# Convolution stage of a four-layer graph kernel: one product in split halves, half of an affine map on another engine

## What is computed

```python
x = x + batchnorm(out)                       # end of layer 1; out is the array O below
h = relu(layernorm(x))
h = relu(einsum('ts,bsh->bth', adj, h @ Wg0 + bg0))
h = relu(einsum('ts,bsh->bth', adj, h @ Wg1 + bg1))
...                                          # then the LSTMs over windows, and layer 3
```

## Time and profile before

| | |
|---|---|
| median of three runs | 1221.98 us (1221.71 to 1222.08) |
| profiled execution: its time, its span | 1222.5 us, 1220.8 us |
| busy in the whole span: PE, DVE, ACT, POOL | 97%, 80%, 74%, 35% |
| this stage | from about 319 us to about 466 us of the span |
| busy from 384 to 424 us: PE, DVE, ACT, POOL | 40.00, 34.79, 34.76, 18.43 of 40 us |

### The profile page before, as it was taken

The page is one execution under the profiler, slowest core; times in us unless marked ns, Lnnn a source line. Parts: engine busy times, 40 slices in busy tenths (PEclk is TensorE's granted clock), DMA queues, the critical chain, the costliest instruction groups (busy, mean ns, idle before and its releaser), DMA issues.

```text
span 1220.8 us, 22403 instructions
## 1 busy us (share of the span) xinstructions
PE 1186.0 (97%) x7262; PEld 1023.4 (84%) x7262; DVE 980.9 (80%) x2005; ACT 901.9 (74%) x1733; POOL 428.2 (35%) x794
## 2 busy tenths in 40 slices
PE   8999999989999998999999999999999999989998
PEld 8999988843688886689888988898898899978997
DVE  6888859977688876888788878887887899987774
ACT  5766779978578876877787768776776688875554
POOL 5878748700276430000000000000000377757764
PEclk9999999999999999999999999999999999999999
DMA  8000000000311100000000000000300030001112
GB/s 322 1 2 2 1 1 1 0 1 0 112 62 69 69 35 1 1 1 1 1 1 1 2 1 1 1 1 1 138 1 1 2 139 2 2 1 51 72 70 87
DMA packets 14924, 38.23 MB, mean 31 GB/s; under 512 B 1904, under 2 KB 3952, under 8 KB 13808
## 3 DMA queue, kind: packets, MB, share of 16 engines
q1 hardware_dynamic: 14000, 36.60, 7.9%
q10 hardware_dynamic: 832, 0.46, 0.1%
HBM read 20.27 MB, written 16.78 MB: 30 GB/s over the span
## 4 chain that ended last, share of the span: by engine, by line
PE 53%; DVE 5%; ACT 2%; issue 1%; POOL 1%; POOLq 0%; DVEq 0%; ACTq 0%
PE psum L1197 7%; PE psum L1198 7%; PE psum L1199 7%; PE psum L1216 5%; PE psum L1212 4%; PE psum L1213 4%; PE psum L1484 2%; PE psum L1736 2%; PE psum L1701 2%; PE psum L1490 2%; PE psum L1711 2%; ACT gates L1235 2%; PE psum L1503 1%; PE psum L1504 1%; PE psum L1722 1%; PE psum L1366 1%
## 5 line engine op out<-in xcount | busy, mean ns | idle before, releaser
L1235 ACT ACTIVATE gates<-psum,lstm_bias 128x512 f32<-128x512 f32 (+1 forms) x504 | 302.2, 637 | 101.8 <-PE psum L1216 88.3
L143 POOL TENSOR_TENSOR l2r_sum<-l2r_st 128x8 f32<-128x8 f32 x16 | 5.2, 323 | 518.0 <-DVE l2r_st L116 517.7
L175 ACT ACTIVATE l_h<-X,nmr,rstd 128x128 f32<-128x128 f32 (+1 forms) x392 | 160.6, 484 | 14.6 <-POOLq L169 14.6
L1198 PE MATMUL psum<-lstm_node_hi,Wih_lo 128*128 128x512 f32 (+1 forms) x408 | 148.3, 363 | 0.0
L1197 PE MATMUL psum<-lstm_node_hi,Wih_hi 128*128 128x512 f32 (+1 forms) x408 | 148.1, 363 | 0.0
L1199 PE MATMUL psum<-lstm_node_lo,Wih_hi 128*128 128x512 f32 (+1 forms) x408 | 148.0, 363 | 0.0
L1212 PE MATMUL psum<-lstm_hid_hi,Whh_hi 128*128 128x512 f32 (+1 forms) x288 | 104.7, 363 | 3.9 <-DVE lstm_hid_hi L1295 3.8
L1216 PE MATMUL psum<-lstm_hid_lo,Whh_hi 128*128 128x512 f32 (+1 forms) x288 | 108.0, 375 | 0.0
L1213 PE MATMUL psum<-lstm_hid_hi,Whh_lo 128*128 128x512 f32 (+1 forms) x288 | 103.6, 360 | 0.0
L1240 ACT ACTIVATE gates<-lstm_cell 128x512 f32<-128x512 f32 (+1 forms) x144 | 83.7, 581 | 21.0 <-DVE lstm_cell L1282 20.6
L1197 PEld LDWEIGHTS psum<-lstm_node_hi,Wih_hi 128*128 128x128 f32 x408 | 77.3, 190 | 10.9 <-ACT gates L1235 0.3
(11 more groups left out here) (277 smaller groups left out, 3456.9 us busy)
## 6 DMA issues: line engine op xcount, KB each, us to landing
x_spill<-X SPq DMA_DIRECT2D x32, 256.0 KB, 2.0
X<-x_spill SPq DMA_DIRECT2D x2, 4096.0 KB, 12.3
out<-X SPq DMA_DIRECT2D x32, 256.0 KB, 2.0
X<-in_x SPq DMA_DIRECT2D x6, 1024.0 KB, 15.3
X<-in_x SPq DMA_DIRECT2D x3, 512.0 KB, 8.7
w_raw<-in_WihT SPq DMA_DIRECT2D x1, 1024.0 KB, 5.6
w_raw<-in_WhhT SPq DMA_DIRECT2D x1, 1024.0 KB, 7.8
X<-in_x SPq DMA_DIRECT2D x2, 256.0 KB, 3.2
```

The source lines that it names most:

```text
L175: last = act.activation(h[:, j, :], k.X[:, bass.ds(b0, TB), :][:, j, :], ACT.Relu, bias=k.nmr[:, bass.ds(b0, TB)][:, j:j + 1], scale=k.rst ...
L1198: pe.matmul(out, lo, x_high, start=False, stop=False)
L1235: act.activation(gate_of(it, g), k.bank[4 * s + g][:, 0:it.N], ACT.Tanh if g == GATE_G else ACT.Sigmoid, bias=k.lstm_bias[:, it.p - 1, g:g ...
```

## The change

ACT reads psZ and writes Z_hi (float32r); DVE, in the place where it copied Z, now subtracts: Z_lo = psZ - Z_hi. DVE splits Wg0 once ahead of its steps. PE takes three float32r calls in place of the one float32 call of L974. `fetch` of the odd tiles moves from ACT to a tensor_scalar on POOL, which goes one turn ahead of the coefficients; POOL's turns are all written out, and it waits for the LSTM weights behind the coefficients of a turn and not ahead of them.

```diff
--- before.py
+++ after.py
@@ -860,11 +860,13 @@
     sem = lambda n: k.sem(n)
     sb = lambda n: ctx.enter_context(nc.sbuf_tensor(n, [P, TB, P], F32))
     h = each(S, lambda s: sb(f"l2_h{s}"))
-    Z, Gb, G, V2 = (sb(f"l2_{n}") for n in ("Z", "Gb", "G", "V2"))
+    Gb, G, V2 = (sb(f"l2_{n}") for n in ("Gb", "G", "V2"))
+    Z_hi, Z_lo = (ctx.enter_context(nc.sbuf_tensor(f"l2_{n}", [P, TB, P], F32R)) for n in ("Z_hi", "Z_lo"))
+    Wg_hi, Wg_lo = (ctx.enter_context(nc.sbuf_tensor(f"l2_{n}", [P, P], F32R)) for n in ("Wg_hi", "Wg_lo"))
     shift = ctx.enter_context(nc.sbuf_tensor("l2_shift", [P, P], F32))
 
-    h_done, Zp_done, Z_done, Gp_done, Gb_done, G_done, V2p_done, V2_done, Hp_done, H_done, sums_done = (
-        sem(f"l2_{n}") for n in ("h", "Zp", "Z", "Gp", "Gb", "G", "V2p", "V2", "Hp", "H", "sums"))
+    h_done, Zp_done, Zhi_done, Wg_split, Z_done, Gp_done, Gb_done, G_done, V2p_done, V2_done, Hp_done, H_done, sums_done = (
+        sem(f"l2_{n}") for n in ("h", "Zp", "Zhi", "Wg", "Z", "Gp", "Gb", "G", "V2p", "V2", "Hp", "H", "sums"))
 
     w_raw = each(2, lambda n: ctx.enter_context(nc.sbuf_tensor(f"w_raw{n}", [P, 4, 4 * P], F32)))
     w_in, w_copied, w_tally = each(2, lambda n: sem(f"lstm_w_in{n}")), sem("w_copied"), sem("w_tally")
@@ -897,16 +899,25 @@
         def _(pool):
             res.ln.open(pool)
             bn_pool(pool)
+            pool.wait_ge(bn_ready, 1)
             zeros = k.zero[:, 0:1].unsqueeze(2).broadcast_to([P, 1, 4 * P])
-            for n, W in enumerate((k.Wih, k.Whh)):
-                pool.wait_ge(w_in[n], 16)
-                with pool.Fori(4 * n, 4 * n + 4) as i:
-                    res.coefficients(pool, i)
-
-                    at = bass.ds(i - 4 * n, 1)
-                    split_float32(pool, w_raw[n][:, at, :], W[0][:, at, :], W[1][:, at, :], w_copied, i + 1, w_tally, zeros)
-            with pool.Fori(8, n_it) as i:
+
+            def fetch(i):
+                if i:
+                    pool.wait_ge(res.R_ready[1], i)
+                pool.tensor_scalar(res.o[1][:, :], O[:, (i * S + 1) * TW:(i * S + 2) * TW], coef[:, 0, 0:1], coef[:, 0, 1:2],
+                                   ALU.mult, ALU.add).then_inc(res.o_ready[1], 1)
+
+            fetch(0)
+            for i in range(n_it):
+                if i + 1 < n_it:
+                    fetch(i + 1)
                 res.coefficients(pool, i)
+                for n, W in enumerate((k.Wih, k.Whh)):
+                    if 4 * n <= i < 4 * n + 4:
+                        pool.wait_ge(w_in[n], 16)
+                        at, count = bass.ds(i - 4 * n, 1), i + 1
+                        split_float32(pool, w_raw[n][:, at, :], W[0][:, at, :], W[1][:, at, :], w_copied, count, w_tally, zeros)
 
         @block.sync
         def _(sp):
@@ -922,7 +933,7 @@
         def _(act):
             def step(i, s, place):
                 t = i * S + s
-                if there(t + FETCH):
+                if there(t + FETCH) and (s + FETCH) % S == 0:
                     q, turn = (s + FETCH) % S, i + (s + FETCH) // S
                     if since(t + FETCH, S):
                         act.wait_ge(res.R_ready[q], turn)
@@ -940,6 +951,11 @@
                 if there(t - 1):
                     act.wait_ge(Gb_done, t - 1 + 1)
                     act.activation(G[:, :, :], Gb[:, :, :], ACT.Relu).then_inc(G_done, 1)
+                if there(t):
+                    act.wait_ge(Zp_done, t + 1)
+                    if since(t, 1):
+                        act.wait_ge(Gp_done, t)
+                    act.activation(Z_hi[:, :, :], as_tile(psZ), ACT.Copy).then_inc(Zhi_done, 1)
 
             act.wait_ge(bn_ready, 1)
             steps(act, step)
@@ -970,8 +986,12 @@
                     pe.wait_ge(G_done, t - 2 + 1)
                     product(psV2, G, k.Wg[:, 1, :], V2p_done)
                 if there(t - 1):
+                    if isinstance(t, int) and t == 1:
+                        pe.wait_ge(Wg_split, 2)
                     pe.wait_ge(Z_done, t - 1 + 1)
-                    pe.matmul(psG[:, :], k.Wg[:, 0, :], Z[:, :, :], start=True, stop=True).then_inc(Gp_done, 1)
+                    pe.matmul(psG[:, :], Wg_hi[:, :], Z_hi[:, :, :], start=True, stop=False)
+                    pe.matmul(psG[:, :], Wg_lo[:, :], Z_hi[:, :, :], start=False, stop=False)
+                    pe.matmul(psG[:, :], Wg_hi[:, :], Z_lo[:, :, :], start=False, stop=True).then_inc(Gp_done, 1)
                 if there(t):
                     pe.wait_ge(h_done, t + 1)
                     product(psZ, h[s], k.adjT[:, :], Zp_done)
@@ -998,14 +1018,15 @@
                     dve.tensor_tensor(Gb[:, :, :], as_tile(psG), shift[:, :].unsqueeze(1).broadcast_to([P, TB, P]),
                                       ALU.add).then_inc(Gb_done, 1)
                 if there(t):
-                    dve.wait_ge(Zp_done, t + 1)
-                    dve.tensor_copy(Z[:, :, :], as_tile(psZ)).then_inc(Z_done, 1)
+                    dve.wait_ge(Zhi_done, t + 1)
+                    dve.tensor_tensor(Z_lo[:, :, :], as_tile(psZ), Z_hi[:, :, :].bitcast(F32), ALU.subtract).then_inc(Z_done, 1)
 
             bn_dve(dve)
             dve.tensor_tensor(k.lstm_bias[:, :, :].rearrange("h p g -> h (p g)"), k.cols[:, C_BIH:C_BIH + 16],
                               k.cols[:, C_BHH:C_BHH + 16], ALU.add)
             dve.wait_ge(sums_done, 1)
             dve.tensor_scalar(shift[:, :], psS[:, 0:P], k.cols[:, C_BG0:C_BG0 + 1], None, ALU.mult).then_inc(sums_done, 1)
+            split_float32(dve, k.Wg[:, 0, :], Wg_hi[:, :], Wg_lo[:, :], Wg_split, 1).then_inc(Wg_split, 1)
             dve.wait_ge(sums_done, 2)
             steps(dve, step)
```

## The result

| | before | with the change |
|---|---|---|
| median (runs) | 1221.71 us (5) | 1241.41 us (1240.21 to 1242.96, 5) |
| ratio to before, 95% interval | | 1.0162 [1.0151, 1.0173] |
| profiled execution: time, span | 1222.5, 1220.8 us | 1240.41, 1238.7 us |

What follows compares the result with a forecast made beforehand. TensorE (PE) was taken to bound the kernel at 3.97 us a tile, with a DVE-ACT loop of 4.74 us replacing it. 22.3 us late after the long part, less 0.9 at the end, gives +21.4: 1243.4 us, range 1238.5 to 1249.

Steps and rivals of the forecast that it cites:

- The loop: DVE's Z_lo to Gb, ACT's G and Z_hi, back to Z_lo: seven links, 4.74 us a step; chance 0.86.
- PE's gain: Wg0 product on PE: three float32r calls, 0.69 us for 0.86; PE's step 3.97 to 3.80 us, 5.4 us alone.
- fetch on POOL: Odd tiles' fetch: 1.26 us on POOL, bounds 1.04 to 2.14; free in the steady part, not at the start.
- The start: First tiles: two fetches on POOL delay the statistics of tile 6 to 344.62, so Z_lo(3) comes 3.96 us late.
- The end: Last tiles, path through PE: 3.53 us a tile, even with before; about 0.9 us back behind the last Z.
- PE busy about 80%: Steady part of the changed profile: PE busy about 80%, waiting about 0.9 us in each tile, in pieces.
- The clock: TensorE's clock: read as full in every slice before, expected to stay full with PE waiting in pieces.
- The bounds: Range of the loop case: 3.6 us either side for the loop, 1.8 up or 0.4 down for fetch; 1238.5 to 1249.
- DVE idle about 1.2 us per tile, ended by Z_hi: Sign in the changed profile: DVE waits ahead of Z_lo for ACT's Z_hi, about 1.2 us each tile.
- PE as the bound: Rival: Z_hi need not wait behind G, so PE's 3.80 us sets the pace; 1216.6 us; chance 0.04.
- POOL in PE's place: Rival without the loop: POOL's 8.33 us turn sets the pace in the first turns; 1224.1 us; chance 0.04.
- POOL slower than the loop: Rival: fetch costs over 2.4 us, so POOL's turn passes 9.48 us; at 3.9, 1258 us; chance 0.04.

Runs made afterwards that it cites:

- e1: The whole change, but ACT takes Z_hi(t) ahead of G(t-1): 1223.27 us, ratio 1.0011.
- e4: The whole change, but DVE takes the statistics of tile t+4 behind Gb(t-1), directly ahead of Z_lo(t): 1217.22 us, ratio 0.9963.
- e7: The whole change plus one extra ACT instruction per tile between G(t-1) and Z_hi(t): 1257.21 us, ratio 1.0287.
- e8: The whole change plus the same extra ACT instruction per tile, but ahead of the normalisation: 1242.71 us, ratio 1.0165.
- e3: The change without its POOL part (fetch of all tiles on ACT, POOL's program as before): 1240.62 us, ratio 1.0155.
- e6: As e4, but fetch is back on ACT for all tiles and POOL's program is that of before: 1217.82 us, ratio 0.9966.
- e5: The whole change, but DVE takes both addition and statistics of tile t+4 behind Gb(t-1), ahead of Z_lo(t): 1222.78 us, ratio 1.0008.
- e9: As e4, but POOL splits the LSTM weight slices in turns 3 to 10, not 0 to 7: 1217.53 us, ratio 0.9969.
- e2: The kernel before with only the POOL part (fetch of odd tiles on POOL, turns written out): 1222.35 us, ratio 1.0004.
- e10: The kernel before with LSTM weight slices split in POOL's turns 3 to 10, turns written out: 1222.28 us, ratio 1.0005.

## Why the prediction was right, point by point

- *The loop.* Right in mechanism and size: 4.71 to 4.72 us measured, 4.74 forecast, all seven links within 0.03. e1 and e4 opened the loop, e7 lengthened it and e8 worked beside it, and each moved the step, or left it, as the loop says.
- *PE's gain is not realised.* Right: e3 holds it and is 19 us slower; e4 and e6, without the loop, show it, 3.98 to 3.81 us a step. e1 shows that an open loop alone isn't enough: there the path through PE and ACT keeps 3.95.
- *fetch on POOL.* Without cost in the steady part, as forecast. The term of the start was mis-sized: 0.78 us measured where 1.26 was taken, which lies under the stated lower end of 1.04 too; the row of that lower end has two input tiles, and fetch has one. The 256-column row of 1069 ns that I let speak against a faster price has its input and output in one tile and immediate operands; the 452 ns row times four would have been worse still. The Trainium skill, page "GPSIMD Engine Reference", section "4.1 Engine selection", calls one-input operations roughly line-rate; 0.78 us is nearer to that (DVE's spacing is 0.60) than my slope was. No run tells why the 128x256 instruction costs more.
- *The start.* Z of tile 3 came 2.9 us late where 4.0 were forecast, and not by the path named: DVE waited for Z_hi of tile 1, not for POOL ahead of the statistics of tile 6 (above). That the size came near is partly luck, since 0.4 us from ahead of the stage, which no term had, made up for part of the surplus.
- *The end.* Forecast 3.53 us a step, measured (479.34 - 464.86) / 4 = 3.62: the product behind a wait took some 0.1 more than the three spacings.
- *PE busy about 80%.* True of the spacing of calls, false of the view that I named.
- *The clock.* It stayed full from 384 to 424 us, as expected (1.00). But "in every slice" reads too much into the earlier trace rows: a 9 stands for 0.9 and more, and the kernel before has 0.91 over the 40 us behind this stage (last section).
- *The bounds.* The terms give 1243.4 - 3.6 - 0.4 = 1239.4 as the lower end; the 1238.5 written there does not follow from them. The 1241.41 lies inside either.
- *DVE idle about 1.2 us per tile, ended by Z_hi; the strict order on ACT.* Seen: 1.18 us. The Trainium skill, page "TensorE: Matmul & The Clock Gate", section "Architectural detail: the array is 16× 32×32, not 1× 128×128", has ScalarE take its queue in order. The trace agrees: ACT stood idle for 0.87 us ahead of G with Z_hi's input complete, and e1 got the time back by changing the order in the program.
- *The rivals.* PE as the bound and POOL in PE's place: excluded by the waits, by e1 and by e3. POOL slower than the loop: excluded by the 0.78 us.

What stays open: the profiled executions differ by only 17.9 us where the stage grew by 20.2. The missing 2.3 us lie in the LSTM stage, see the last section. The medians, of five runs each, differ by 19.7.

## What to carry to other kernels

Before splitting an instruction over two engines, write down the program order of both and look for a path that leaves an engine and comes back to it in the same step; its length, not the engines' busy shares, bounded the step here. If there is one, find work on the waiting engine that neither end of the path needs and put it in the gap, and then look for the loop that this makes (e5). A copy inserted at the idle spot and at the suspected spot (e7, e8) settles such a question in two runs.

## What the runs showed of the hardware

TensorE's clock fell to its lower level (1.2 GHz) for some microseconds after this stage in eleven of the twelve profiles; with the change, float32r calls then started 0.43 us apart and not 0.23. PE had been idle for 2.33 us ahead of the first product of the LSTM stage (2.61 in e7 and e8), with gaps of 0.2 to 0.6 and of 0.8 us shortly before. In e9, with gaps of 0.46, 0.78 and 2.33 us, the clock did not fall. The windows view, 40 us from the start of the LSTM stage (the clock is the third number from the end), in the kernel before and in e9:

```profile
466.30:506.30 40.00, 33.66 (x127) 25.54 (x128) 31.73 (x52) 32.54 (x56) 0.00 (x0) 0.91 0.00 1
```

```profile
462.40:502.40 40.00, 34.01 (x140) 25.87 (x141) 34.66 (x58) 34.59 (x60) 0.00 (x0) 1.00 0.00 1
```

All twelve profiles, by that clock and by the time from the first x_hi of that stage to the last:

| clock over the 40 us | profiles | first to last x_hi, us |
|---|---|---|
| 1.00 | e9 | 385.9 |
| 0.96 | the change, e3, e5 | 387.1, 387.1, 387.4 |
| 0.91 | before, e1, e2, e7, e10 | 389.4, 388.9, 388.4, 388.7, 389.4 |
| 0.87 | e4, e6, e8 | 389.3, 389.1, 389.2 |

From 1.00 to 0.91 the time grows as the clock falls, and 0.87 adds nothing to it. Before and the change differ by 0.05 x 40 us = 2.0 us of granted clock and by 2.4 us of time, which fits the 2.3 us above. It would also explain the spread of some 3 us between runs of one kernel, but each kernel has one profile and no run isolated the cause.
